# Token centring and the restoring product on quarters of the array, low band summed in PSUM

## The chip, the cores and the metric

The kernel runs on one core of one Trainium2 chip. The metric is device time in microseconds. Several runs of a kernel are given by their median; one further execution is taken by the profiler, and its trace is what the rows below are read from.

## The reference

Input x is (4, 64, 128, 128): batch, channel, height, width. Two blocks are computed, each a convolution part and a token part, each with a residual:

```python
x = x + L0_conv(_ln_c(x))          # Haar wavelet mixer        <- the stage that the change touches
t = to_tokens(x)
t = t + L0_ffn(_ln_t(t))           # expert-choice top-8 MoE   <- its gate logits come from the same stage
x = from_tokens(t)
x = x + L1_conv(_ln_c(x))          # four directional scans
t = to_tokens(x)
t = t + L1_ffn(_ln_t(t))           # top-2 mixture
```

`_ln_c` and `_ln_t` both normalise over the 64 channels of a pixel (eps 1e-6 and 1e-5). `L0_conv` takes the Haar transform of each 2x2 block into four bands, scales each by exp(s) per channel, projects the 256 band channels to 64 (w1, b1), projects back to 256 (w2, b2) and inverts the transform. The Haar transform, the scales and w1 are one linear map of the four pixels to the low projection (`Alow`); w2 and the inverse are another, back to the four pixels (`Brec`). With the weights that reach the kernel, the restored value depends on the row and column parity of the pixel.

## The kernel before

The image is cut into 64 chunks. A chunk is a tile of 128 partitions by 512 columns: partition halves t=0,1 are even and odd image rows, 64 channels each; columns are 4 row pairs by 128 pixels, so even and odd columns v=0,1 are neighbours. Per chunk `wavelet_mixer` does:

- `centre`: x split in two fp32r parts, times the centring matrix `Cm` (block diagonal: a 64x64 block for each half) into PSUM `xc`; `square` (ScalarE), split again (VectorE, GpSimd); `variance`: times `J` (1/64 in two diagonal blocks) into `va`; `log_of_variance`, `rstd` (ScalarE); `normalise` (VectorE) gives `nn`.
- `low`: for v=0,1, `Alow[:, v]` (128x64) times the columns of parity v, 256 of them. The two results lie in the two partition halves of bank `tv`, not yet summed; `copy_low` adds b1 (zero in the second half) and moves both to `lowS` (128x256).
- `restore`: for v=0,1, `Brec[:, v]` (128x128, both partition halves alike, so the product also sums the two parts of low) times `lowS` into `rec`. `add_restored` (VectorE, two instructions) adds it and b2 to x: the chunk then holds x1.
- `token_centre` (full `Cm` times x1 into `tc`) and `token_square` (ScalarE, into `tsq`); `turn` (four transposes of x1) and `copy_tokens` (VectorE), which is stored as token rows.
- Per pair of chunks `gate_logits` (into `lg`), `token_variance` (into `tv`, on column halves), `token_rstd` (two ScalarE instructions), `scale_logits` and `block_top` (VectorE).

f32 matmuls appear as two instructions each in the trace, fp32r ones as one.

All engines execute in order, in the order written out in the source; semaphores join them. Step c of the loop mixes chunks of different age. The order on each engine (in parentheses the lag, and "odd" for what stands only in odd steps):

- TensorE (455-469): centre(c), variance(c-1), low(c-2), odd: gate_logits and token_variance, then token_centre(c-3), turn(c-3), restore(c-2).
- ScalarE (508-520): square(c), log(c-1), copy_low(c-2), rstd(c-1), odd: token_rstd, then token_square(c-3).
- VectorE (588-602): add_restored(c-3), high_of_square(c), high_of_x(c+2), scale_logits or block_top, normalise(c-1), copy_tokens(c-3).
- GpSimd: low_of_square(c), low_of_x(c+2). SP: loads three steps ahead, stores of x1 and tokens.

`centre(c)` waits for `normed` of chunk c-2 (two `xc` banks); `copy_tokens` waits for `turn`; `low` and `token_variance` share bank `tv`. One loop over steps 0 to 68 runs them; odd steps are long, even ones short.

Of the kernel before, what the change touches and what calls it, by code (L numbers as in the profile page):

```python
# [30 lines left out]
P = 128  # L31
# [144 lines left out]
def setup_block0(nc, g, a):  # L176

    with ExitStack() as ctx:
# [21 lines left out]
        with nc.Block() as block:  # L200
            @block.sync
            def _(sp):
                def load(dst, src, sem):
                    sp.dma_start(dst, src, allow_slow_non_contiguous=True).then_inc(sem, 16)

                for h in range(2):
                    part = slice(h * C, h * C + C)
                    load(w2n[part, :, 0:C], a["w2"].rearrange("(j c) o -> c j o", j=4), loaded)
                    load(w1n[:, :, h], a["w1"].rearrange("o (j c) -> o j c", j=4), loaded)
                    load(gwn[:, h], a["gate_w"], loaded)  # L210
                for c in range(AHEAD):
                    for t in range(2):
                        sp.dma_start(g.xr[c][t * C:t * C + C].rearrange("p (j w) -> p j w", j=JR),
                                     x_chunk(a, c, t)).then_inc(g.xin[c], 16)
                load(g.b1[0:C], a["b1"].rearrange("(c o) -> c o", o=1), g.late_loaded)
                for q in range(4):
                    load(g.gate_b[q * E0:q * E0 + E0, :], a["gate_b"].rearrange("(e o) -> e o", o=1), g.late_loaded)
                load(g.w2bias, a["weight2"][:, HID:HID + 1, :].rearrange("e h o -> e (h o)"), g.late_loaded)
# [9 lines left out]
            def _(dve):  # L228
# [4 lines left out]
                dve.memset(g.eps[:, 0:1], EPS_C)  # L233
                dve.memset(g.eps[:, 1:2], EPS_T)
                dve.memset(gtb[:], 0.0)
                dve.memset(g.b1[C:P], 0.0)
                dve.memset(g.E[:, TOK:TOK + PAD], SENTINEL)
                dve.memset(sg[0:C], 1.0)
                dve.memset(sg[C:P], -1.0)
# [80 lines left out]
def wavelet_mixer(nc, g, a):  # L320
# [3 lines left out]
    with ExitStack() as ctx:  # L324
        m = Mem(nc, ctx, "wm")
        xc = [m.ps("xc0"), m.ps("xc1")]
        va, rec, tc, tt, lg, tv = (m.ps(n) for n in ("va", "rec", "tc", "tt", "lg", "tv"))
        xin, x1_out, tok_out = g.xin, m.sems("x1o", XBUFS), m.sems("tko", 4)
        s = {n: m.sem(n) for n in (
            "centred", "squared", "var", "lnv", "rstd", "normed", "low", "low_s", "rec", "x1",  # L330
# [11 lines left out]
        def now(c):  # L342

            return 0 <= c < CHUNKS

        def buf(c):

            return xr[c % XBUFS]

        with nc.Block() as block:  # L350
            @block.sync
            def _(sp):
                def load(c):
                    wait(sp, x1_out[c % XBUFS], c // XBUFS * 16)
                    wait(sp, s["tturned"], c - XBUFS + 1)
                    wait(sp, s["logits"], (c - XBUFS) // 2 * 2 + 2)
                    for t in range(2):
                        sp.dma_start(buf(c)[t * C:t * C + C].rearrange("p (j w) -> p j w", j=JR),
                                     x_chunk(a, c, t)).then_inc(xin[c % XBUFS], 16)

                def load_experts(q):

                    e = slice(q * E0 // 8, (q + 1) * E0 // 8)
                    sp.dma_start(g.W1[0:C + 1, e], a["weight1"][e].rearrange("e d h -> d e h")
                                 ).then_inc(g.experts_loaded, 16)
                    for t in range(2):
                        sp.dma_start(g.W2[:, e, t, :], a["weight2"][e, t * P:t * P + P, :].rearrange(
                            "e p o -> p e o")).then_inc(g.experts_loaded, 16)

                def store_x1(c):  # L370
                    wait(sp, s["x1"], c + 1)
                    sp.dma_start(g.x1s[c:c + 1].rearrange("t p n -> p (t n)"), buf(c)).then_inc(x1_out[c % XBUFS], 16)

                def store_tokens(c):
                    wait(sp, s["tcopied"], c + 1)
                    sp.dma_start(tok_dst[c % B][:, c // B * JR:c // B * JR + JR, :],
                                 ts[c % 4].rearrange("p (j x) -> p j x", j=JR)).then_inc(tok_out[c % 4], 16)

                for sem in g.setup_sems:
                    sp.sem_clear(sem)  # L380
                for c in steps:
                    if now(c + AHEAD):
                        load(c + AHEAD)
                    if 8 <= c < 16:
                        load_experts(c - 8)
                    if now(c - 3):
                        store_x1(c - 3)
                    if now(c - 4):
                        store_tokens(c - 4)
                for u in range(XBUFS):  # L390
                    sp.wait_ge(x1_out[u], 16 * len(range(u, CHUNKS, XBUFS)))
                for u in range(4):
                    sp.wait_ge(tok_out[u], 16 * (CHUNKS // 4))
                sp.wait_ge(g.late_loaded, 16 * 6)

            @block.tensor
            def _(pe):
# [14 lines left out]
                def low(c):  # L412
                    wait(pe, s["normed"], c + 1)
                    wait(pe, s["low_s"], c)
                    wait(pe, s["tln"], (c - 2) // 2)
                    nv = nn[c % 2].rearrange("p (q v) -> p v q", v=2)
                    for v in range(2):
                        last = pe.matmul(tv[v * C:v * C + C, 0:N // 2], g.Alow[:, v], nv[:, v], start=True, stop=True)
                    last.then_inc(s["low"], 1)

                def gate_logits(pair):
# [6 lines left out]
                def token_variance(pair, c):  # L428
                    wait(pe, s["tsquared"], 2 * pair + 2)
                    wait(pe, s["low_s"], min(c + 1, CHUNKS))  # L430
                    for half in range(2):
                        last = pe.matmul(tv[half * C:half * C + C, :], g.J[:, C - E0:C + E0], tsq[half],
                                         start=True, stop=True)
                    last.then_inc(s["tvar"], 2)

                def token_centre(c):
                    wait(pe, s["x1"], c + 1)
                    wait(pe, s["tsquared"], c)
                    pe.matmul(tc[:], g.Cm[:], buf(c), start=True, stop=True).then_inc(s["tcentred"], 1)

                def turn(c):
                    wait(pe, s["tcopied"], c)
# [4 lines left out]
                def restore(c):  # L447
                    wait(pe, s["low_s"], c + 1)
                    wait(pe, s["x1"], c)
                    for v in range(2):  # L450
                        last = pe.matmul(rec[:, v * (N // 2):(v + 1) * (N // 2)], g.Brec[:, v], lowS[c % 2],
                                         start=True, stop=True)
                    last.then_inc(s["rec"], 1)

                for c in steps:
                    if now(c):
                        centre(c)
                    if now(c - 1):
                        variance(c - 1)
                    if now(c - 2):  # L460
                        low(c - 2)
                    if now(c - 4) and c % 2 == 1:
                        gate_logits((c - 4) // 2)
                        token_variance((c - 4) // 2, c - 2)
                    if now(c - 3):
                        token_centre(c - 3)
                        turn(c - 3)
                    if now(c - 2):
                        restore(c - 2)
# [2 lines left out]
            def _(act):  # L472
# [15 lines left out]

                def copy_low(c):
                    if c == 0:  # L490
                        act.wait_ge(g.late_loaded, 16 * 6)
                    wait(act, s["low"], c + 1)
                    wait(act, s["rec"], c - 1)
                    act.activation(lowS[c % 2], tv[:, 0:N // 2], ACT.Identity, bias=g.b1[:]).then_inc(s["low_s"], 1)

                def token_rstd(pair):
                    wait(act, s["tvar"], 2 * pair + 2)
# [4 lines left out]

                def token_square(c):
                    wait(act, s["tcentred"], c + 1)
                    wait(act, s["tvar"], c - 1)
                    act.activation(tsq[c % 2], tc[:], ACT.Square).then_inc(s["tsquared"], 1)

                for c in steps:
                    if now(c):
                        square(c)  # L510
                    if now(c - 1):
                        log_of_variance(c - 1)
                    if now(c - 2):
                        copy_low(c - 2)
                    if now(c - 1):
                        rstd(c - 1)
                    if now(c - 4) and c % 2 == 1:
                        token_rstd((c - 4) // 2)
                    if now(c - 3):
                        token_square(c - 3)  # L520

            @block.gpsimd
            def _(pool):
# [18 lines left out]
            def _(dve):  # L542
# [6 lines left out]

                def add_restored(c):  # L550
                    wait(dve, s["rec"], c + 1)
                    xv = buf(c).rearrange("p (q v) -> p v q", v=2)
                    for v in range(2):
                        last = dve.scalar_tensor_tensor(xv[:, v], rec[:, v * (N // 2):(v + 1) * (N // 2)],
                                                        g.b2c[:, v:v + 1], xv[:, v], ALU.add, ALU.add)
                    last.then_inc(s["x1"], 1)

# [1192 lines left out]
def metaformer_kernel(nc, a, out):  # L1750
    g = Shared()
    with ExitStack() as ctx:
# [18 lines left out]

        v = Views(g.X, 0)
        g.xr = [v.take(N) for _ in range(XBUFS)]
        g.sq, g.rr, g.nn, g.tsq = ([v.take(N) for _ in range(2)] for _ in range(4))
        g.lowS = [v.take(N // 2) for _ in range(2)]
        g.ts = [v.take(N) for _ in range(4)]
        g.trs = v.take(N)
        v = Views(g.X, 2 * (TOK + PAD))
# [58 lines left out]
```

## Time and profile before

| | us |
|---|---|
| median of 3 runs (lowest, highest) | 2211.32 (2211.24, 2211.95) |
| time of the profiled execution | 2214.93 |
| its span, which the rows are relative to | 2213.0 |
| TensorE busy in the span | 2096.7 |

The wavelet stage lies between 15 and 336 us of the span. Three more stages follow (expert choice, four scans, mixture). A row of a timeline begins with the start in us and the duration in us of the instruction or of xN merged instructions; consecutive instructions of an engine overlap in their records, so the distance from start to start is often less than a duration.

### The profile page before, as it was taken

What the parts mean: (1) busy time and instruction counts of PE and PEld (TensorE: products, weight loads), DVE (VectorE), ACT (ScalarE), POOL (GpSimd) and SP (SyncE); (2) the same over time, 40 slices, a digit from 0 to 9 for tenths busy, and PEclk for the clock granted to TensorE, in tenths of its full rate; (3) what the DMA queues carried; (4) which work ended last, traced back from release to release, by engine and by line L of the source; (5) the groups of instructions that cost most, each with busy time, mean ns of one, the idle gap of its engine ahead of it and who ended that gap; (6) DMA issues with size and microseconds to landing.
All of it is one profiled execution on the core that took longest, in us unless ns stands there. A gap on an engine that the chain in (4) does not pass through costs nothing. (4 is left out here: it accounts for less than half of the span.)

```text
span 2213.0 us, 40957 instructions
## 1 busy us (share of the span) xinstructions
PE 2096.7 (95%) x14474; PEld 1611.6 (73%) x14474; DVE 1273.2 (58%) x2621; ACT 1037.5 (47%) x2879; POOL 590.6 (27%) x644
## 2 busy tenths in 40 slices
PE   6999991799999989999999999999996999999999
PEld 3555550477777789999999999999994555555554
DVE  4777778566666633222222222222226999999998
ACT  4666664344444313333444444444445455454451
POOL 4555534222222200000000000000006655656561
PEclk9999995699999999999999999999996999999999
DMA  4955540222223200000000000000004555555543
GB/s 114 240 166 163 167 142 22 91 86 93 90 96 96 68 12 0 0 0 0 4 0 0 0 0 0 0 0 0 0 0 118 129 131 131 132 131 130 128 117 77
DMA packets 176417, 159.06 MB, mean 72 GB/s; under 512 B 25976, under 2 KB 126360, under 8 KB 176280
## 3 DMA queue, kind: packets, MB, share of 16 engines
q1 hardware_dynamic: 174584, 156.91, 26.1%
q8 instruction: 61, 1.00, 0.2%
q0 software_dynamic: 512, 0.53, 0.1%
q14 instruction: 76, 0.62, 0.1%
q10 hardware_dynamic: 1184, 0.00, 0.0%
HBM read 56.72 MB, written 67.11 MB: 56 GB/s over the span
## 5 line engine op out<-in xcount | busy, mean ns | idle before, releaser
L1194 PE MATMUL s_ps<-g_ring,g_T 128*128 128x128 f32 x7620 | 855.4, 274 | 7.6 <-DVE g_ring L1237 7.6
L1194 PEld LDWEIGHTS s_ps<-g_ring,g_T 128*128 128x128 f32 x7620 | 854.5, 191 | 8.3 <-DVE g_ring L1237 8.1
L1226 DVE SCALAR_TENSOR_TENSOR g_ring<-s_ps,s_xs 128x128 f32<-128x128 f32 x508 | 148.3, 292 | 421.3 <-PE s_ps L1194 421.3
L1574 POOL TENSOR_TENSOR g_X<-tm_x,g_X 128x512 f32<-128x512 f32 x64 | 83.4, 1325 | 869.0 <-DVE tm_m L1654 869.0
L1282 ACT ACTIVATE g_X<-g_ring 128x256 f32<-128x256 f32 x254 | 172.2, 678 | 294.2 <-DVE g_ring L1226 294.2
L1663 DVE TENSOR_TENSOR tm_Z<-tm_pg,tm_nd 128x1024 f32<-128x1024 f32 x256 | 299.0, 1209 | 10.1 <-PE tm_pg L1457 10.0
L1469 PE MATMUL tm_po<-tm_Z,g_wexp 128*64 128x512 f32 x1024 | 247.7, 605 | 0.0
L1266 ACT ACTIVATE g_X<-g_ring 64x256 f32 x256 | 106.8, 417 | 205.6 <-DVE g_ring L1226 203.3
L1226 DVE SCALAR_TENSOR_TENSOR g_ring<-s_ps,g_X 128x128 f32<-128x128 f32 x254 | 74.0, 292 | 211.0 <-PE s_ps L1194 211.0
L1277 ACT ACTIVATE s_xs<-g_X 128x256 f32<-128x256 f32 x254 | 161.4, 637 | 0.6 <-PEq L1176 0.6
L1457 PE MATMUL tm_pg<-tm_gT,tm_sel 96*128 96x512 f32 x512 | 146.9, 408 | 1.1 <-DVE tm_Z L1663 1.0
L1469 PEld LDWEIGHTS tm_po<-tm_Z,g_wexp 128*64 128x64 f32 x1024 | 62.2, 136 | 108.5 <-issue 99.8
L997 PEld LDWEIGHTS af_ps<-g_yh,g_Tlo 128*128 128x128 f32 x635 | 85.0, 189 | 66.7 <-DVE g_yh L1108 54.2
L526 POOL TENSOR_TENSOR wm_sql<-g_X,wm_sqh 128x512 fp32r<-128x512 f32 x64 | 89.2, 1394 | 134.3 <-DVE wm_sqh L561 133.1
L997 PE MATMUL af_ps<-g_yh,g_Tlo 128*128 128x256 f32 x635 | 111.5, 306 | 5.9 <-DVE g_yh L1108 4.2
L1578 POOL TENSOR_TENSOR tm_xl<-g_X,tm_xh 128x512 fp32r<-128x512 f32 x64 | 82.9, 1296 | 98.8 <-ACT tm_xh L1503 98.7
L1457 PEld LDWEIGHTS tm_pg<-tm_gT,tm_sel 96*128 96x128 f32 x512 | 92.6, 190 | 20.4 <-issue 4.1
L1108 DVE SCALAR_TENSOR_TENSOR g_yh<-af_ps,g_X 128x256 fp32r<-128x256 f32 x127 | 54.0, 426 | 90.5 <-PE af_ps L1001 87.8
L1511 ACT ACTIVATE tm_nS<-tm_bankA 128x512 f32<-128x512 f32 x64 | 38.2, 596 | 140.9 <-PE tm_bankA L1424 140.9
L1001 PE MATMUL af_ps<-g_yl,g_Thi 128*128 128x256 f32 x635 | 99.2, 288 | 0.0
L997 PE MATMUL af_ps<-g_yh,g_Thi 128*128 128x256 f32 x635 | 97.9, 285 | 0.0
L1526 ACT ACTIVATE tm_bankA<-tm_bankA 128x64 f32<-128x64 f32 x256 | 53.4, 220 | 88.5 <-PE tm_bankA L1436 88.5
(279 smaller groups left out, 3140.4 us busy)
## 6 DMA issues: line engine op xcount, KB each, us to landing
tm_nd<-tm_nS SPq DMA_DIRECT2D x256, 128.0 KB, 2.4
g_X<-in_x SPq DMA_DIRECT2D x128, 128.0 KB, 3.0
x1s<-g_X SPq DMA_DIRECT2D x64, 256.0 KB, 2.1
x1tok<-g_X SPq DMA_DIRECT2D x64, 256.0 KB, 2.5
tm_x<-x2s SPq DMA_DIRECT2D x64, 256.0 KB, 2.9
y<-tm_yo SPq DMA_DIRECT2D x128, 128.0 KB, 2.5
g_X<-x1s SPq DMA_DIRECT2D x32, 256.0 KB, 2.8
x2s<-g_X SPq DMA_DIRECT2D x32, 256.0 KB, 2.0
```

What stands on the lines that cost most here:

```text
L526: pool.tensor_tensor(sq_lo[:], sq[c % 2], sq_hi[:].bitcast(F32), ALU.subtract).then_inc(s["parts"], 1)
L997: pe.matmul(out, t[:, d * P:d * P + P], g.yh[:, :, d:d + 64], start=(t is g.Tlo and d == 0), stop=False)
L1001: last = pe.matmul(out, g.Thi[:, d * P:d * P + P], g.yl[:, :, d:d + 64], start=False, stop=(d == ND - 1))
L1194: last = pe.matmul(out, g.T[i][:, d * P:d * P + P], g.ring[(u - 1) % RING][:, images(c), d:d + 64], start=(d == 0), stop=(d == ND - 1))
L1226: dve.scalar_tensor_tensor(g.ring[n % RING][:, images(c), inner], conv, 0.0, x[:, images(c)], ALU.max, ALU.add).then_inc(y_ready[c], 1)
L1266: last = act.activation(dst.rearrange("p b j w -> p b (j w)"), src, ACT.Copy)
L1277: act.activation(xs[n % RING][:], line(*place(n)), ACT.Copy).then_inc(staged, 1)
L1282: act.activation(line(*place(n)), g.ring[n % RING][:, :, inner], ACT.Copy).then_inc(stored, 1)
L1457: last = pe.matmul(pg[q % 2][:, h * N:h * N + N], sel[:, at:at + 2].rearrange("p e c -> p (e c)"), gT[i][:], start=True, stop=True)
L1469: last = pe.matmul(po[i][h * C:h * C + C, :], wexp[:, ep], Z[q % 4][:, h], start=False, stop=(ep == EP - 1), skip_group_check=True)
L1574: pool.tensor_tensor(xv, natural(x2[t % 2][i][:]), xv, ALU.add).then_inc(s["x3"], 1)
L1663: dve.tensor_tensor(Z[q % 4][:], pg[q % 2][:].rearrange("p (h n) -> p h n", h=2), nd[t % 2][i][:], ALU.mult).then_inc(s["z"], 1)
```

## The change

`token_centre` and `restore` issue 64x64 quarters; `low` sums over v in PSUM, with the column half h in the partitions, so `lowS` is 128x128; `rec` and `tc` share two banks (row groups write different banks). `token_variance` then has 16 instructions on 32-column strips. `tsq` has four buffers for two. On TensorE `token_centre` moves ahead of `low`, on ScalarE `token_square` moves ahead of `copy_low`.

```diff
-                load(g.b1[0:C], a["b1"].rearrange("(c o) -> c o", o=1), g.late_loaded)
+                for h in range(2):
+                    load(g.b1[h * C:h * C + C], a["b1"].rearrange("(c o) -> c o", o=1), g.late_loaded)
...
-                dve.memset(g.b1[C:P], 0.0)
...
-        va, rec, tc, tt, lg, tv = (m.ps(n) for n in ("va", "rec", "tc", "tt", "lg", "tv"))
+        va, tt, lg, tv = (m.ps(n) for n in ("va", "tt", "lg", "tv"))
+
+        both = m.ps("rt", (P, 2 * N))[:].rearrange("p (r k n) -> p r k n", r=2, k=2)
+        rec, tc = both[:, :, 0], both[:, :, 1]
...
                 def low(c):
...
-                    nv = nn[c % 2].rearrange("p (q v) -> p v q", v=2)
+                    nv = nn[c % 2].rearrange("p (h q v) -> p h v q", h=2, v=2)
                     for v in range(2):
-                        last = pe.matmul(tv[v * C:v * C + C, 0:N // 2], g.Alow[:, v], nv[:, v], start=True, stop=True)
+                        for h in range(2):
+                            last = pe.matmul(tv[h * C:h * C + C, 0:N // 4], g.Alow[:, v], nv[:, h, v],
+                                             start=(v == 0), stop=(v == 1))
...
                 def token_variance(pair, c):
-                    for half in range(2):
-                        last = pe.matmul(tv[half * C:half * C + C, :], g.J[:, C - E0:C + E0], tsq[half],
-                                         start=True, stop=True)
+                    for h in range(2):
+                        of_half = g.J[:, h * C:h * C + E0]
+                        for half in range(2):
+                            for t in range(2):
+                                at = half * C + t * E0
+                                last = pe.matmul(tv[at:at + E0, h * (N // 2):(h + 1) * (N // 2)], of_half,
+                                                 tsq[(2 * pair + half) % 4][:, t * (N // 2):(t + 1) * (N // 2)], start=True, stop=True)
...
                 def token_centre(c):
-                    pe.matmul(tc[:], g.Cm[:], buf(c), start=True, stop=True).then_inc(s["tcentred"], 1)
+                    src = buf(c).rearrange("p (h n) -> p h n", h=2)
+                    for t, h in ((0, 0), (1, 1), (0, 1), (1, 0)):
+                        rows = slice(t * C, t * C + C)
+                        last = pe.matmul(tc[h * C:h * C + C, t], g.Cm[rows, rows], src[rows, h], start=True, stop=True)
+                    last.then_inc(s["tcentred"], 1)
...
                 def restore(c):
                     wait(pe, s["low_s"], c + 1)
                     wait(pe, s["x1"], c)
+                    wait(pe, s["tsquared"], c)
                     for v in range(2):
-                        last = pe.matmul(rec[:, v * (N // 2):(v + 1) * (N // 2)], g.Brec[:, v], lowS[c % 2],
-                                         start=True, stop=True)
+                        for h, t in ((0, 0), (1, 1), (0, 1), (1, 0)):
+                            rows = slice(h * C, h * C + C)
+                            last = pe.matmul(rec[t * C:t * C + C, h, v * (N // 4):(v + 1) * (N // 4)],
+                                             g.Brec[rows, v, t * C:t * C + C], lowS[c % 2][rows], start=True, stop=True)
...
+                    if now(c - 3):
+                        token_centre(c - 3)
                     if now(c - 2):
                         low(c - 2)
                     if now(c - 4) and c % 2 == 1:
                         gate_logits((c - 4) // 2)
                         token_variance((c - 4) // 2, c - 2)
                     if now(c - 3):
-                        token_centre(c - 3)
                         turn(c - 3)
...
-                    act.activation(lowS[c % 2], tv[:, 0:N // 2], ACT.Identity, bias=g.b1[:]).then_inc(s["low_s"], 1)
+                    act.activation(lowS[c % 2], tv[:, 0:N // 4], ACT.Identity, bias=g.b1[:]).then_inc(s["low_s"], 1)
...
                 def token_square(c):
-                    wait(act, s["tvar"], c - 1)
-                    act.activation(tsq[c % 2], tc[:], ACT.Square).then_inc(s["tsquared"], 1)
+                    wait(act, s["tvar"], c - 3)
+                    act.activation(tsq[c % 4].rearrange("p (t n) -> p t n", t=2), tc, ACT.Square
+                                   ).then_inc(s["tsquared"], 1)
...
+                    if now(c - 3):
+                        token_square(c - 3)
                     if now(c - 2):
                         copy_low(c - 2)
                     if now(c - 1):
                         rstd(c - 1)
                     if now(c - 4) and c % 2 == 1:
                         token_rstd((c - 4) // 2)
-                    if now(c - 3):
-                        token_square(c - 3)
...
                 def add_restored(c):
-                    xv = buf(c).rearrange("p (q v) -> p v q", v=2)
+                    xv = buf(c).rearrange("p (h q v) -> p v h q", h=2, v=2)
                     for v in range(2):
-                        last = dve.scalar_tensor_tensor(xv[:, v], rec[:, v * (N // 2):(v + 1) * (N // 2)],
+                        last = dve.scalar_tensor_tensor(xv[:, v], rec[:, :, v * (N // 4):(v + 1) * (N // 4)],
                                                         g.b2c[:, v:v + 1], xv[:, v], ALU.add, ALU.add)
```

The views of the shared array X follow (`tsq` four tiles, `lowS` two of 128 columns), and two waits for the late loads count seven loads for six.

## Rows read from the trace of the kernel before

**Rows 1.** Page part 1, and windows of the stage: busy us of each engine, clock, DMA.

```profile
PE 2096.7 (95%) x14474; PEld 1611.6 (73%) x14474; DVE 1273.2 (58%) x2621; ACT 1037.5 (47%) x2879; POOL 590.6 (27%) x644
...
34.60:314.80 280.20, 280.20 (x1297) 156.30 (x1295) 209.42 (x411) 192.60 (x353) 154.28 (x118) 1.00 0.62 179
```

**Rows 2.** Timeline of TensorE over one pair of steps: start, duration, instruction.

```profile
148.91 0.58 PE L403 MATMUL wm_xc<-wm_xh,wm_Cmr 128*128 128x512 f32 x1
...
152.80 0.58 PE L403 MATMUL wm_xc<-wm_xh,wm_Cmr 128*128 128x512 f32 x1
...
153.45 0.39 PE L409 MATMUL wm_va<-wm_sqh,g_J 128*128 128x512 f32 x1
...
153.69 0.40 PE L410 MATMUL wm_va<-wm_sql,g_J 128*128 128x512 f32 x1
154.01 0.67 PE L418 MATMUL wm_tv<-g_X 128*64 128x256 f32 x4
...
154.52 1.02 PE L425 MATMUL wm_lg<-g_X 128*64 128x512 f32 x4
...
155.37 1.06 PE L432 MATMUL wm_tv<-g_X,g_J 128*64 128x512 f32 x4
...
156.36 1.13 PE L439 MATMUL wm_tc<-g_X,g_Cm 128*128 128x512 f32 x2
...
157.32 0.60 PE L444 MATMUL wm_tt<-g_X 128*128 128x128 f32 x4
...
158.44 0.58 PE L403 MATMUL wm_xc<-wm_xh,wm_Cmr 128*128 128x512 f32 x1
```

**Rows 3.** Timeline of VectorE and ScalarE in the same pair.

```profile
151.87 0.69 DVE L566 TENSOR_TENSOR g_X<-wm_xc,g_X 128x512 f32<-128x512 f32 x1
...
152.47 0.68 DVE L571 COPY g_X<-wm_tt 128x512 f32<-128x512 f32 x1
...
153.19 0.88 DVE L554 SCALAR_TENSOR_TENSOR g_X<-wm_rec,g_b2c,g_X 128x256 f32<-128x256 f32 x2
...
153.65 0.60 ACT L478 ACTIVATE g_X<-wm_xc 128x512 f32<-128x512 f32 x1 [1.17 <-PE wm_xc L404]
...
154.15 0.69 ACT L483 ACTIVATE g_X<-wm_va,g_eps 128x512 f32<-128x512 f32 x1
...
154.73 0.48 ACT L494 ACTIVATE g_X<-wm_tv,g_b 128x256 f32<-128x256 f32 x1
...
155.10 0.62 ACT L487 ACTIVATE g_X<-g_X 128x512 f32<-128x512 f32 x1
```

**Rows 4.** Timeline of the next stage around 64x64 quarters, weight loads (PEld) last.

```profile
500.42 0.40 PE L1031 MATMUL af_dl<-af_sql,g_J 128*128 128x512 f32 x1
500.75 0.68 PE L1021 MATMUL af_xc<-g_X,g_Cm 64*64 64x256 f32 x8
501.36 0.88 PE L997 MATMUL af_ps<-g_yh,g_Tlo 128*128 128x256 f32 x5
502.07 0.77 PE L997 MATMUL af_ps<-g_yh,g_Thi 128*128 128x256 f32 x5
502.68 0.78 PE L1001 MATMUL af_ps<-g_yl,g_Thi 128*128 128x256 f32 x5
...
500.75 0.21 PEld L1021 LDWEIGHTS af_xc<-g_X,g_Cm 64*64 64x64 f32 x8 [0.36 <-issue]
```

**Rows 5.** Expert stage: 32-column matmuls, and the window with its granted clock.

```profile
381.96 7.05 PE L881 MATMUL ec_psh<-g_X,ec_pT 65*32 65x256 f32 x64 [0.42 <-ACT ec_pT L808]
...
382.00:398.00 16.00, 14.30 (x208) 9.47 (x208) 15.96 (x5) 4.36 (x7) 7.79 (x4) 0.51 0.11 35
```

**Rows 6.** Timeline at the stage's end: a token centring that waits for VectorE.

```profile
328.92 0.88 DVE L554 SCALAR_TENSOR_TENSOR g_X<-wm_rec,g_b2c,g_X 128x256 f32<-128x256 f32 x2 [0.17 <-PE wm_rec L451]
...
329.85 1.12 PE L439 MATMUL wm_tc<-g_X,g_Cm 128*128 128x512 f32 x2 [0.97 <-DVE g_X L554]
```

**Rows 7.** Timeline of ScalarE at the stage's start: the first copy_low.

```profile
27.33 0.47 ACT L494 ACTIVATE g_X<-wm_tv,g_b 128x256 f32<-128x256 f32 x1 [0.43 <-PE wm_tv L418]
```

More of the change, by code:

```diff
@@ L393, in _ @@
                     sp.wait_ge(tok_out[u], 16 * (CHUNKS // 4))
-                sp.wait_ge(g.late_loaded, 16 * 6)
+                sp.wait_ge(g.late_loaded, 16 * 7)
             @block.tensor
@@ L490, in copy_low @@
                     if c == 0:
-                        act.wait_ge(g.late_loaded, 16 * 6)
+                        act.wait_ge(g.late_loaded, 16 * 7)
                     wait(act, s["low"], c + 1)
                     wait(act, s["rec"], c - 1)
-                    act.activation(lowS[c % 2], tv[:, 0:N // 2], ACT.Identity, bias=g.b1[:]).then_inc(s["low_s"], 1)
+                    act.activation(lowS[c % 2], tv[:, 0:N // 4], ACT.Identity, bias=g.b1[:]).then_inc(s["low_s"], 1)
                 def token_rstd(pair):
@@ L1773, in metaformer_kernel @@
         g.xr = [v.take(N) for _ in range(XBUFS)]
-        g.sq, g.rr, g.nn, g.tsq = ([v.take(N) for _ in range(2)] for _ in range(4))
-        g.lowS = [v.take(N // 2) for _ in range(2)]
+        g.sq, g.rr, g.nn = ([v.take(N) for _ in range(2)] for _ in range(3))
+        g.tsq = [v.take(N) for _ in range(4)]
+        g.lowS = [v.take(N // 4) for _ in range(2)]
         g.ts = [v.take(N) for _ in range(4)]
```

## The prediction

> **What bounds the kernel now.** The page comes first: TensorE is busy for 95% of the span [rows 1]. The windows then cut out the wavelet stage. From 34.6 to 314.8 us TensorE is busy for all 280.20 us, VectorE for 209.42, ScalarE for 192.60, GpSimd for 154.28 [rows 1]. So the array is the limit there and no other engine is. Next comes the timeline of TensorE. It repeats one pair of steps: a short one (148.91 to 152.80, 3.89 us) and a long one with the logits and the token variance (152.80 to 158.44, 5.64 us), 9.53 us together [rows 2]. Steps 4 to 63 are 30 such pairs, 286 us. Last I read ScalarE and VectorE in the same pair [rows 3], because once the array is shorter their order may be the next limit.
>
> **What the change takes off TensorE.** The logits are four matmul instructions of 512 columns that go two by two on the column halves, each in two passes: four pass times in 0.85 (154.52 to 155.37) [rows 2], 0.213 each. An f32 product on the full array takes four passes. The short step thus streams for 0.853 (centre and variance, one pass for each of four instructions) + 0.427 (low) + 0.853 (token centring) + 0.427 (turn) + 0.853 (restore) = 3.41; the long step 1.71 more, 5.12.
>
> Four 64x64 quarters at once halve the columns: 0.427 for the token centring. The next stage already does this very operation (L1021, 64*64, 64x256, x8), with 0.61 to the next start [rows 4], where the full one has 0.96 (156.36 to 157.32) [rows 2]. So quarters do run side by side. `restore` becomes sixteen 64*64 matmuls of 128 columns, 0.427 in place of 0.853. `low` issues eight for four, with the same columns. `token_variance` issues sixteen for four on 32-column strips, each strip 2x256 columns: 0.853 as before. L881, 64 matmuls of 32x256 in 7.05 us at a granted clock of 0.51 [rows 5], is 0.110 each, 0.055 at full clock; sixteen give 0.88. Streaming falls to 2.56 and 4.27.
>
> **What it adds on TensorE: changes of shape.** L1021 starts 0.33 after the last full matmul, where 0.235 is usual (153.45 to 153.69); the group stands for 0.18 over its streaming; and the five matmuls behind it take 0.71 where the next five take 0.61 [rows 2, 4]. In and out together cost 0.09+0.18+0.10 = 0.37 to 0.39, some 0.19 per change. Today a step has two changes. Afterwards it has five: to quarters (token centring), to column halves (low), to full (turn), to quarters (restore), to full; the long step has a sixth if 32-column strips count as another shape.
>
> In the new order of TensorE the short step is centre and variance 1.14 (4x0.235, +0.09 on leaving, +0.11 behind quarters), token centring 0.61, low 0.60 (the long step's 0.51 to a group of its own shape and 0.09 to another), turn 0.65 (0.427 and a change on either side), restore 0.61: 3.61. The long one has 0.51+0.85+0.99 for low, logits and token variance [rows 2] in place of 0.60: 5.36. A sixth change makes it 5.55; if changes between two tiled shapes are free it is 5.15. I take 5.36, since most of the changes are of the kind that [rows 4] shows.
>
> The Trainium skill, "TensorEngine Tiling (Array Packing)", section Key Properties, says that changing the tiling mode drains the array. [...]
>
> **What it moves: a ring closes.** Token centring now stands before `low`, and `token_square` before `copy_low` and `rstd` on ScalarE, where it was last. This makes a ring: x1 of a chunk, token centring, token square, copy_low, rstd, normalise, copy_tokens, add_restored, which is x1 of the next chunk. All of it lies within one step. With x1 at 0:
> - hop from VectorE's add to the centring 0.05 (328.92+0.88 to 329.85) [rows 6]; quarters to their end 0.68 [rows 4]; hop of the same size: square at 0.78.
> - ScalarE would be free at 0.78+0.50 (square to log, 153.65 to 154.15) [rows 3], 1.28. But `low` starts 0.61 behind the centring and ends 0.67 later [rows 2, 4], at 1.33; hop 0.05 (154.68 to 154.73) [rows 2, 3]: copy_low at 1.38.
> - copy_low: log (512 columns) 0.69 and copy_low (256) 0.48 have the same bias operand and give 0.82 ns a column [rows 3], so 0.37 for 128. Its successor starts 0.11 before its end [rows 3]: rstd at 1.64, and 0.62 later it ends, 2.26.
> - hop 0.05: normalise 2.31; copy_tokens 0.60 later, add 0.60 later (151.87 to 152.47 for an instruction of that length) [rows 3], 3.51; its two halves 0.88 [rows 3]: 4.39.
>
> The short step can't be under 4.39, though TensorE could do it in 3.61; it is 3.89 now. Queued behind the waiting centring on TensorE are low, turn and restore, and ScalarE's two copies wait with them; behind the waiting normalise stand copy_tokens and the add. The add reads PSUM in runs of 128 instead of 256, same elements: nothing, at most 0.05. Bounds for the ring: 4.25 if `low` doesn't gate and the hops shrink, 4.55 if split operands and eight weight loads slow it. `centre` of the next step also awaits this normalise (end 3.00), and centre plus variance then last until 4.14, just under 4.39.
>
> In the long step copy_tokens waits for `turn`, behind the token variance. From turn's start VectorE needs 0.60+0.05+0.60+0.88+0.05 = 2.18, TensorE 0.55+0.61+1.14 = 2.30, so TensorE sets it, at 5.36; were it quicker by over 0.12, VectorE would be next.
>
> The rest: restore's new wait for the token square adds nothing, as the square precedes the copy_low that restore awaits anyway. Four `tsq` buffers for two, one memset less: nothing. One more tiny load of b1 ahead of gate_b in SP's queue: the first copy_low comes at 27.33 [rows 7], long after; nothing.
>
> **Sum.** Pair: 4.39+5.36 = 9.75 against 9.53, +0.22; times 30, +6.6 us. At the start the first restores, issued alone, get shorter; at the end the last short steps, which have no centre, wait for the same ring. I set these against each other, with 1 us either way. The profiled execution has a span of 2213.0 and a time of 2214.93; it would give 2221.5. The median of the runs is 3.6 under it, so the forecast is 2211.3+6.6 = **2217.9**.
>
> **Rivals.**
> - A, no difference that shows (within 0.2%, 4.4 us, about what a measurement of this kernel can tell): changes between adjoining tiled shapes are free (long step 5.15) and the ring is 4.30 to 4.45. The pair is 9.45 to 9.60, the time 2209 to 2213. For it: only changes between full and tiled are in the trace. Against it: leaving quarters slows even the matmuls behind them.
> - B, faster: the ring doesn't bind, since some member has slack that I took for order. The pair is 3.61+5.36 = 8.97, -0.56 times 30: 2194; half of it, 2203. Against it: every member awaits the one before or follows it on its engine. It decides once the ring is under 4.0.
> - C, much slower: the sixteen loads and matmuls of restore don't overlap in the array and it keeps its 0.853. The long step is 0.43 more, 30 times: 2231. It decides if sixteen short ones behave otherwise than L1021's eight, whose loads lie within 0.21 us [rows 4].
> - D, the ring at 4.55 and the sixth change: pair 10.1, 2228.
>
> The Trainium skill, "TensorE: Matmul & The Clock Gate", section LDWEIGHTS, times a load by its columns over 1.2 GHz, 53 ns for 64. Sixteen in a row would be 0.85, which is C's size; that section doesn't say whether loads of different quarters share the time, and eight in 0.21 us say they do.
>
> **How the numbers follow.** Forecast 0.45, with a range of its own from 2213.5 to 2223; A 0.27; B 0.17; C 0.05; D 0.06. The range for 8 in 10 is 2205 to 2229: all of A and D, and only the mildest of B. Faster by over 0.2% (below 2206.9) is B with a trace of A, 0.18. Within 0.2% is A and the low edge of the forecast, 0.28. Slower 0.54.
>
> **What would show it.** Token centring as 64*64 x8 in about 0.6 us and restore as sixteen in the same; in every short step TensorE idle before token centring, released by VectorE's add, 0.2 to 0.6 us, and no such idle in long steps; copy_low at about 0.37 us, started by `low`. A short step clearly under 4.2 refutes the ring; a long step near 5.15 or 5.55 settles the changes of shape; restore above 0.8 shows that it doesn't overlap. The other stages must not move: if they do, or if the granted clock of this stage leaves 1.00, the forecast fails for another reason.

## The result

The changed kernel takes 2220.69 us (median of 5 runs, 2220.02 to 2223.28), the kernel before 2211.32 (5 runs, 2210.19 to 2213.92). The ratio is 1.0041, 95% interval 1.0029 to 1.0053: slower, by 9.4 us where 6.6 were forecast.

The page and the windows of the profile after (for windows: length, busy us of PE, PEld, DVE, ACT, POOL, granted clock, DMA share, GB/s):

```profile
PE 2073.7 (93%) x16266; PEld 1595.2 (72%) x16266; DVE 1268.6 (57%) x2620; ACT 1036.6 (47%) x2879; POOL 591.0 (27%) x644
...
34.60:314.80 280.20, 258.65 (x2868) 142.19 (x2872) 200.82 (x403) 188.08 (x346) 151.73 (x116) 1.00 0.62 178
```

TensorE is busy for 23 us less and the kernel is slower. In the stage it is no longer full: 258.65 of 280.20 us, against 280.20 [rows 1]. The clock of the stage did not move.

One short and one long step of TensorE, the timeline after (start, duration, instruction):

```profile
152.58 0.66 PE L451 MATMUL wm_rt<-g_X,g_Cm 64*64 64x256 f32 x8
...
153.17 0.67 PE L422 MATMUL wm_tv<-g_X 128*64 128x128 f32 x8
...
155.65 0.47 PE L406 MATMUL wm_xc<-wm_xh,wm_Cmr 128*128 128x512 f32 x1 [0.62 <-DVE g_X L584]
...
156.42 0.40 PE L413 MATMUL wm_va<-wm_sql,g_J 128*128 128x512 f32 x1
...
156.94 0.66 PE L451 MATMUL wm_rt<-g_X,g_Cm 64*64 64x256 f32 x8
...
158.04 1.03 PE L430 MATMUL wm_lg<-g_X 128*64 128x512 f32 x4
...
159.00 1.07 PE L441 MATMUL wm_tv<-g_X,g_J 128*32 128x256 f32 x16
...
160.00 0.66 PE L457 MATMUL wm_tt<-g_X 128*128 128x128 f32 x4
...
160.59 0.67 PE L467 MATMUL wm_rt<-g_X 64*64 64x128 f32 x16
...
161.18 0.50 PE L406 MATMUL wm_xc<-wm_xh,wm_Cmr 128*128 128x512 f32 x1
...
161.98 0.40 PE L413 MATMUL wm_va<-wm_sql,g_J 128*128 128x512 f32 x1
...
162.31 0.66 PE L451 MATMUL wm_rt<-g_X,g_Cm 64*64 64x256 f32 x8
```

From token centring to token centring the short step is 4.36 us (152.58 to 156.94), the long one 5.37 (to 162.31). The pair is 9.73 against 9.53 [rows 2]: 30 times +0.20 is 6.0 us. Start to start, token centring stands at 0.59 where the full one stood at 0.96 [rows 2]. Restore stands at 0.59 for 0.427 of streaming, so its sixteen matmuls do run side by side; what the quarters of restore gain once the changes of shape are paid is told below. Most of the rest of the stage's loss is at its end, also told below.

The members of the ring in that short step, VectorE and ScalarE, and the weight loads of the next token centring:

```profile
153.31 0.60 ACT L523 ACTIVATE g_X<-wm_rt 128x512 f32<-128x512 f32 x1
...
153.89 0.37 ACT L511 ACTIVATE g_X<-wm_tv,g_b 128x128 f32<-128x128 f32 x1
...
154.16 0.62 ACT L504 ACTIVATE g_X<-g_X 128x512 f32<-128x512 f32 x1
...
154.81 0.69 DVE L584 TENSOR_TENSOR g_X<-wm_xc,g_X 128x512 f32<-128x512 f32 x1 [0.60 <-ACT g_X L504]
155.42 0.68 DVE L589 COPY g_X<-wm_tt 128x512 f32<-128x512 f32 x1
...
156.02 0.87 DVE L572 SCALAR_TENSOR_TENSOR g_X<-wm_rt,g_b2c,g_X 128x256 f32<-128x256 f32 x2
...
156.94 0.21 PEld L451 LDWEIGHTS wm_rt<-g_X,g_Cm 64*64 64x64 f32 x8 [0.56 <-DVE g_X L572]
```

Square, copy_low (0.37), rstd, normalise, copy_tokens, add, and the token centring 0.05 behind the add's end. In every short step TensorE waits twice: `centre` waits 0.62 for normalise (155.65), and the token centring waits for the add. That second wait is 0.19: from the last variance to the token centring it is 0.52 (156.42 to 156.94), in the long step 0.33 (161.98 to 162.31). The forecast had put the whole idle time, 0.2 to 0.6 us, before the token centring; the larger part lies before `centre`, at the ring's own normalise. The bracket of a weight load is no sign by itself: in the long step it names the same add.

```profile
162.31 0.21 PEld L451 LDWEIGHTS wm_rt<-g_X,g_Cm 64*64 64x64 f32 x8 [0.36 <-DVE g_X L572]
```

### The profile page after: what moved, and what is told of

It is laid out like the page before. It is cut to its first block and busy times, and to the rows that moved or that the text cites. A ratio compares the mean times of both kernels' runs of the same rounds, so it can differ in the third digit from the quotient of the medians.

```text
span 2218.8 us, 44539 instructions
## 1 busy us (share of the span) xinstructions
PE 2073.7 (93%) x16266; PEld 1595.2 (72%) x16266; DVE 1268.6 (57%) x2620; ACT 1036.6 (47%) x2879; POOL 591.0 (27%) x644
```

## The experiments

Steps are read as above (token centring to token centring; centre to centre in the kernels with token centring behind low). The last column but one is where the last block_top of the stage starts in the profiled execution. Each ratio is to runs of the kernel before on the same chip. Where an expectation says "the first experiment", it means the changed kernel with add first.

| kernel | short | long | pair | stage's end | ratio (95%) |
|---|---|---|---|---|---|
| before | 3.89 | 5.64 | 9.53 | 335.4 | 1 |
| changed | 4.36 | 5.37 | 9.73 | 344.3 | 1.0041 (1.0029, 1.0053) |
| before, new order alone | 4.92 | 5.90 | 10.82 | 377.5 | 1.0190 (1.0173, 1.0207) |
| changed, order back | 3.97 | 6.31 | 10.28 | 359.8 | 1.0107 (1.0090, 1.0124) |
| same, square before token_rstd | 3.98 | 5.67 | 9.65 | 338.1 | 1.0011 (1.0002, 1.0021) |
| changed, add first | 4.17 | 5.37 | 9.54 | 336.3 | 1.0007 (0.9998, 1.0017) |
| before, add first | 3.89 | 5.64 | 9.53 | 335.6 | 0.9999 (0.9990, 1.0008) |
| changed, rstd first | 3.99 | 5.68 | 9.67 | 338.3 | 1.0019 (1.0009, 1.0028) |
| changed, rstd and add first | 4.09 | 5.38 | 9.47 | 332.6 | 0.9999 (0.9989, 1.0008) |
| changed, turn early | 4.36 | 5.51 | 9.87 | 348.8 | 1.0062 (1.0046, 1.0077) |
| changed, full restore | 4.46 | 5.55 | 10.01 | 351.7 | 1.0081 (1.0066, 1.0096) |
| add first, variance first | 3.93 | 5.36 | 9.29 | 328.5 | 0.9976 (0.9967, 0.9984) |
| same, rstd first | 3.93 | 5.54 | 9.47 | 333.6 | 1.0002 (0.9993, 1.0010) |

### The new order without the quarters

```diff
 # kernel before, TensorE; likewise token_square ahead of copy_low on ScalarE, and four tsq buffers
+                    if now(c - 3):
+                        token_centre(c - 3)
                     if now(c - 2):
                         low(c - 2)
...
                     if now(c - 3):
-                        token_centre(c - 3)
                         turn(c - 3)
```

> The kernel before with the order move alone: full-array token centring ahead of low, token_square ahead of copy_low, four tsq buffers; no quarters. Ring theory: the ring has the full centring (0.96 to low's start) and the 256-column copy_low (0.37 to its successor): 0.05+0.96+0.67+0.05+0.37+0.62+0.05+0.60+0.60+0.88 = 4.85 for the short step, the long one 5.64; pair 10.5 against 9.53, 30 times +0.96: about 2240. Rival, the quarters and their changes of shape cost the time and the order nothing: 2211.

Measured: 2256.75 us, 42.7 over the runs of before. About 2240 was expected. The short step is 4.92 (4.85 expected). So the order by itself makes the loss, and far more of it with full centring: the quarters earn back most of what the order costs. The long step is 5.90, not 5.64, a miss. There too the token centring waits for the add, and the add for restore's end:

```profile
153.44 1.03 PE L451 MATMUL wm_rec<-g_X 128*128 128x256 f32 x4
...
154.51 0.88 DVE L555 SCALAR_TENSOR_TENSOR g_X<-wm_rec,g_b2c,g_X 128x256 f32<-128x256 f32 x2 [0.17 <-PE wm_rec L451]
...
155.44 1.13 PE L439 MATMUL wm_tc<-g_X,g_Cm 128*128 128x512 f32 x2
```

Restore ends at 154.47, the add runs from 154.51 to 155.39, and the centring starts at 155.44.

### The quarters in the old order

```diff
 # changed kernel: on TensorE token_centre back in front of turn; on ScalarE:
-                    if now(c - 3):
-                        token_square(c - 3)
                     ...copy_low, rstd, token_rstd
+                    if now(c - 3):
+                        token_square(c - 3)
```

> The changed kernel with the order of before on TensorE and ScalarE, quarters kept. Ring theory: the ring opens, but restore now waits for token_square, which in long steps stands behind both token_rstd instructions: token variance's end +0.05+0.72+0.53+0.60 against restore's natural place, a stall of 0.8; short step 3.9 (token_square last, 0.3 stall). Pair 9.9 to 10.0: about 2227, so the move was needed by the shared banks. Rival, the order move is all of the loss: short 3.6, long 5.4 to 5.55, pair 9.1, 2201.

> As the order of before with quarters, but token_square ahead of token_rstd on ScalarE. Ring theory: no ring, small stall of restore for token_square: short step 3.9, long 5.45, pair 9.35, 30 times -0.38 from the changed kernel: about 2209. Rival, order is indifferent and shape changes are the cost: 2221.

Measured: 2238.57 and 2216.24, beside 2214.06 of before. The first is slower than the changed kernel, as expected, by more than expected (about 2227). In the long step restore waits for the token square, which stands behind both halves of token_rstd:

```profile
155.27 0.66 PE L451 MATMUL wm_rt<-g_X,g_Cm 64*64 64x256 f32 x8
155.41 0.69 ACT L515 ACTIVATE g_X<-wm_tv,g_eps 128x512 f32<-128x512 f32 x1 [0.99 <-PE wm_tv L441]
...
156.13 0.63 ACT L517 ACTIVATE g_X<-g_X 128x512 f32<-128x512 f32 x1
...
156.66 0.58 ACT L522 ACTIVATE g_X<-wm_rt 128x512 f32<-128x512 f32 x1
157.38 0.67 PE L467 MATMUL wm_rt<-g_X 64*64 64x128 f32 x16 [0.87 <-ACT g_X L522]
```

Since rec and tc share banks, the old order isn't open to the new layout as it stands. With the square ahead of token_rstd the long step falls from 6.31 to 5.67, and the kernel to 0.1% over before; I expected 5.45 and a gain, and missed what was left of the wait for the square (0.22 in front of restore) and the sixth change of shape. The Trainium skill, "PSUM — Partial Sum Buffer", section PSUM bank collisions raise a hardware error, says that two engines may not use one bank and quadrant at once even at different bytes; no run here shows it. Restore without its wait for the square was therefore not tried, and whether it would pay stays open.

### Which members close the ring

```diff
 # changed kernel, VectorE
-                    if now(c - 3):
-                        add_restored(c - 3)
                     if now(c):
                         high_of_square(c)
...
                         normalise(c - 1)
+                    if now(c - 2):
+                        add_restored(c - 2)
                     if now(c - 3):
                         copy_tokens(c - 3)
```

> The changed kernel with one edit on VectorE: add_restored(c-2) stands behind normalise(c-1) and ahead of copy_tokens(c-3), instead of behind it. Ring theory: copy_tokens' 0.60 leaves the ring; the ring is 3.79 and the short step 3.8 instead of 4.37, the long step stays 5.36 (TensorE). Pair 9.15 against 9.73, 30 times -0.57: about 2203 us, faster than both kernels. Rival, the changes of shape alone make the kernel slower (TensorE bound in both steps): nothing moves, 2221. Rival, another wait of the same length takes over: short step stays above 4.2, 2216 or more.

> Control: the kernel before with VectorE's add_restored(c-2) ahead of copy_tokens(c-3), the edit of the first experiment. TensorE is the limit in both steps of that kernel, so it gains nothing: the same within 0.2%. Rival, this order is better by itself and the first experiment's gain says nothing of a ring: 5 us or more faster than before.

Measured: 2215.5 (10 runs) beside 2214.06, and 2211.61 beside 2211.96. The edit is worth 0.3% on the changed kernel and nothing on the one before, so its gain is the ring's. But the short step is 4.17, not 3.79: the prediction had named the runner-up itself (normalise, centre and variance, token centring: 4.14), and this expectation left it out. The one wait that the waits of TensorE's matmuls in the stage name (who waited for whom, us in total, times, longest):

```profile
PE wm_xc L406 <- DVE g_X L584: 18.6, 30, 0.6
```

30 waits of 0.6 us of the next `centre` for normalise: one for each short step. The changed kernel has the same line; there the token centring then waits 0.19 more for the add, and here it follows the variance at once. So a second ring of 4.17 stood 0.2 us behind the first, and took over.

```diff
 # changed kernel, ScalarE; in the second kernel with the VectorE edit, and copy_low ahead of token_square
                         log_of_variance(c - 1)
+                    if now(c - 1):
+                        rstd(c - 1)
                     ...token_square, copy_low
-                    if now(c - 1):
-                        rstd(c - 1)
```

> The changed kernel with rstd(c-1) moved on ScalarE ahead of token_square(c-3) and copy_low(c-2), in this order; nothing else. Ring theory: both rings lose token square and copy_low, but copy_low now ends 2.24 behind the token centring and restore waits for it: short step 4.03 against 4.37; in the long step token_variance waits for copy_low (shared bank), 5.5 against 5.36. Pair 9.55 to 9.6, about 2216. Rival, the ring goes only through token square and low, and rstd's place is indifferent: 2221.

> The changed kernel with add_restored ahead of copy_tokens on VectorE (as in the first experiment) and, on ScalarE, rstd(c-1) right behind log_of_variance(c-1), then copy_low(c-2), then token_square(c-3). The first experiment's short step was 4.17 instead of 3.79 because a second ring took over: token square, copy_low, rstd, normalise, the next centre, variance, token centring. With rstd early neither ring contains it; what is left is restore waiting for the token square (2.24 behind the centring's start) and then restore 0.60, centre and variance 1.12: short step 4.0, long 5.36, pair 9.4. Second-ring theory: 30 times -0.17 from the 9.54 of the first experiment, 5 us under it, about 0.1 to 0.2% under the kernel before. Rival, TensorE or VectorE is the limit already at 9.54: no change from the first experiment.

Measured: 2214.72 and 2211.84 beside 2211.96. Alone, rstd first gives 3.99 and 5.68 (4.03 and 5.5 expected): both rings shorten, and copy_low, now later, holds up restore and in long steps the token variance. With both edits the pair is 9.47 (9.4 expected); in short steps restore then waits 0.51 for the token square, which stands last. Between the changed kernel and this one nothing but order differs, and the pair goes from 9.73 to 9.47: the order sets the time, and TensorE's sum is only a floor.

### What a change of shape costs

```diff
 # changed kernel, TensorE
+                    if now(c - 3):
+                        turn(c - 3)
                     if now(c - 4) and c % 2 == 1:
                         gate_logits((c - 4) // 2)
                         token_variance((c - 4) // 2, c - 2)
-                    if now(c - 3):
-                        turn(c - 3)
```

> The changed kernel with turn(c-3) ahead of the logits and the token variance in long steps, so that TensorE has one more change of shape there (column halves, full, column halves) and no work more. Theory of the changes of shape: the long step, which TensorE sets, grows by 0.15 to 0.2; short steps stay; 30 times +0.17: about 2226. Rival, changes cost nothing where weight loads can be drawn ahead: 2221. Rival, the long step is set by copy_tokens behind turn on VectorE, which now starts 2 us sooner: below 2219.

> The changed kernel with low, copy_low, restore and add_restored of before (full array, 256-column lowS); token centring stays on quarters, and the order stays. Two changes of shape less, restore's streaming 0.427 more. By the changes of shape as the profile after shows them (0.10 to 0.15 each) the long step grows by 0.13 to 0.23; the short step is the ring, which gets 0.10 longer by copy_low: 4.47. Pair 9.73 + 0.28: 8 us above the changed kernel, 2229. Rival, changes at 0.20 each as forecast: the long step is the same, the pair +0.13, 2225. Rival, quarters of restore are the cost: faster than the changed kernel.

Measured: 2225.49 beside 2211.96, and 2230.35 beside 2211.09. One more change adds 0.14 to the long step and nothing to the short one (4.36), so the long step is TensorE's. With a full restore two changes fall away, 0.427 of streaming returns, and the long step is 0.18 longer, as expected. But that long step is no longer TensorE's alone. The full restore ends later, the add waits for it, and the token centring for the add:

```profile
154.04 1.03 PE L463 MATMUL wm_rt<-g_X 128*128 128x256 f32 x4
...
154.72 0.58 PE L406 MATMUL wm_xc<-wm_xh,wm_Cmr 128*128 128x512 f32 x1
...
155.11 0.88 DVE L567 SCALAR_TENSOR_TENSOR g_X<-wm_rt,g_b2c,g_X 128x256 f32<-128x256 f32 x2 [0.18 <-PE wm_rt L463]
...
155.61 0.40 PE L413 MATMUL wm_va<-wm_sql,g_J 128*128 128x512 f32 x1
...
156.05 0.66 PE L449 MATMUL wm_rt<-g_X,g_Cm 64*64 64x256 f32 x8
```

The add ends at 155.99. From the last variance to the token centring it is 0.44, against the 0.33 of the changed kernel's long step, so 0.11 of the 0.18 is this wait and 0.07 is TensorE's. By this estimate the two changes gave back 0.427 less 0.07, 0.36 us, or 0.18 each, near the 0.19 of the forecast; that the expectation's 0.10 to 0.15 each gave the right step is luck. The added change cost 0.14, of another pair of shapes; whether the kind of change sets its price stays open. So the two changes around restore take back most of what its quarters save in streaming. What is left is 0.07 on TensorE and 0.11 by an earlier end of restore in long steps. The short step is 0.10 longer in this kernel, all of it in copy_low's 256 columns (0.47 for 0.37), which belong to the old form of `low`.

### A version that beats both

```diff
 # add first, and on TensorE
-                    if now(c):
-                        centre(c)
                     if now(c - 1):
                         variance(c - 1)
+                    if now(c):
+                        centre(c)
 # and on ScalarE
-                    if now(c):
-                        square(c)
                     if now(c - 1):
                         log_of_variance(c - 1)
+                    if now(c):
+                        square(c)
```

> The first experiment (add_restored ahead of copy_tokens) with variance(c-1) ahead of centre(c) on TensorE and log_of_variance(c-1) ahead of square(c) on ScalarE. Two-ring theory: the second ring (normalise, centre, variance, token centring) loses the variance, since only centre waits for normalise: normalise ends at 3.00 behind the token centring, centre 0.47+0.1 later gives 3.65; the first ring is 3.79 to 3.84. The split of the square (VectorE, then GpSimd, 1.40) must reach the variance earlier and may hold it until 2.80, which gives 3.9. Short step 3.85 to 3.9 against 4.17, long 5.38: pair 9.25, about 8 us under the first experiment and 0.2 to 0.3% under the kernel before. Rival, GpSimd's part becomes the limit: short step 4.2 or more, no gain over the first experiment.

> As the experiment beside it, but ScalarE in the order log, square, rstd, token_square, copy_low. Neither ring holds token square and copy_low; restore waits for copy_low, 2.18 behind the token centring, and then 0.60+1.12 and the changes of shape: short step 3.95. In long steps the token variance waits for copy_low by 0.1 to 0.2: 5.5. Pair 9.45, as the kernel of rstd first and add first, 3 to 6 us above the experiment beside it. Rival, with variance first ScalarE's order is indifferent: equal to it.

Measured: 2206.75 (11 runs) beside 2211.09, ratio 0.9976 (0.9967 to 0.9984), and 2212.09. The first is 0.24% faster than before and some 0.6% faster than the changed kernel, on the same work. Its short step is 3.93, and what ends it is GpSimd's part of the square's split, which holds variance until 2.81 behind the token centring (156.13 to 158.94; 2.80 expected):

```profile
157.49 1.40 POOL L544 TENSOR_TENSOR wm_sql<-g_X,wm_sqh 128x512 fp32r<-128x512 f32 x1 [2.73 <-DVE wm_sqh L579]
...
158.94 0.50 PE L412 MATMUL wm_va<-wm_sqh,g_J 128*128 128x512 f32 x1 [0.36 <-POOL wm_sql L544]
```

The second kernel has the same short step (3.93; 3.95 expected), where restore now waits 0.29 for copy_low, and loses in the long one (5.54; 5.5 expected), where the token variance waits for the late copy_low.

## Why the prediction was right, step by step

- **The ring.** 4.39 forecast, 4.36 measured, each member at its place. The order move alone (4.92 against 4.85), the order back (no ring) and the add first bear it out. This step carries the sign of the result. TensorE's idle time was foreseen in the wrong place, as told above.
- **The streaming saved.** Quarters at 0.59 to the next start, 0.61 forecast; rival C (no overlap) is out, as restore's sixteen stand at 0.59.
- **Changes of shape.** The long step came out at 5.36 to 5.37 as forecast, in part because errors cancel. Its terms by start to start: logits to token variance stands at 0.96, where 0.85 was taken from the kernel before, so the change to 32-column strips does cost 0.11 and there are six changes and not five. Against it, turn stands at 0.59 for 0.65, and token centring and restore at 0.59 for 0.61 each. Neither rival value of the long step came, 5.15 (A, changes between tiled shapes free) or 5.55 (D, a sixth at full price).
- **VectorE's runner-up in long steps** (0.12 behind) held, though closer than forecast: the add ends at 162.20, 0.11 before the token centring, and with the hop of 0.05 it is some 0.06 behind. With turn early, which frees copy_tokens, the long step did not fall; with a full restore this path took over.
- **The sum's ends.** This is the term that was mis-sized: 0 forecast with 1 us either way, +2.9 in the profile (8.9 less the 6.0 of the pairs). From the last centre to the last block_top it takes 23.3 us (321.0 to 344.3), before 20.7 (314.8 to 335.4); the other 0.3 lies before it. The windows after:

```profile
330.00:333.00 3.00, 1.10 (x14) 0.36 (x12) 2.52 (x5) 0.04 (x1) 0.00 (x0) 0.87 0.09 32
333.00:336.00 3.00, 3.00 (x20) 1.27 (x24) 0.00 (x0) 0.93 (x2) 0.00 (x0) 0.56 0.47 149
336.00:339.00 3.00, 2.00 (x40) 1.11 (x32) 1.70 (x4) 1.32 (x2) 0.00 (x0) 1.00 0.00 0
```

and what TensorE did there:

```profile
331.98 0.94 PE L451 MATMUL wm_rt<-g_X,g_Cm 64*64 64x256 f32 x8 [1.90 <-DVE g_X L572]
...
332.84 1.12 PE L422 MATMUL wm_tv<-g_X 128*64 128x128 f32 x8
...
333.76 1.92 PE L430 MATMUL wm_lg<-g_X 128*64 128x512 f32 x4
...
335.60 1.07 PE L441 MATMUL wm_tv<-g_X,g_J 128*32 128x256 f32 x16
```

The last short step has neither centre nor variance, so TensorE idled for 1.90 us, until the ring's add. From 333 to 336 us the granted clock was 0.56, near the lower of its two levels (1.2 GHz), and token centring, low and logits stood at 0.86+0.92+1.84 where 0.59+0.51+0.96 is usual: 1.6 us. The rest, 1.0 us, goes to the ring itself, in the last short steps (4.36 from 327.62 to 331.98, where the two of the kernel before took 3.4). In the kernel before the same place kept 1.00 (0.97 of idle in front of its last centring [rows 6]). That the idle time caused the drop is inferred; no run varied it alone. The other traces only partly bear it out. With turn early the same place idled for 1.91 us, and the clock of the next 3 us was 0.53. With a full restore it idled for 1.49 and with add first for 1.31, and the clock kept 1.00. But in the quarters with the order back the clock fell to 0.50 behind an idle time of 0.99, after other waits of 0.39 and 0.87 in front of restore. So the length of this one wait doesn't settle it.
- **The stage and the whole.** The stage ends 8.9 us later in the profile, the medians differ by 9.4, but the two spans only by 5.8 (2213.0 and 2218.8). The profiled execution before was itself 3.6 over its median; behind the stage, with the same code in both, the profile after gets 3 us back, 1.4 of it in the first scan (359.1 us from its first to its last convolution, against 360.5). Why these stages vary by that much isn't settled.

Rival B had its worth: a pair under 9.4 is possible (9.29), but only after the ring is opened in two places.

## What to carry to other kernels

When one engine is full, work out what it would take without it: follow each value from its producer back to its own next turn through every engine's order, and write down the second longest ring beside the first, as it stands there once the first is opened. Moving an operation ahead in one engine's order can close such a ring inside one step; here that was worth +1.9% with the operation at full size. Small tiles save streaming time, but count the changes of shape on either side of each group: around restore, two of them took back an estimated 0.36 of the 0.427 us saved.

## What the runs showed of the hardware

- Four 64x64 quarters run side by side, also with sixteen matmuls of 128 columns each and their sixteen weight loads: 0.59 us to the next group's start for 0.427 of streaming.
- One more change between array shapes with no work added cost 0.14 us; two fewer gave back 0.36 by estimate (0.427 of streaming returned, TensorE's part of the step grew by 0.07).
- Sixteen matmuls on 32-column strips, 256 columns each, stood at 1.00 us (159.00 to 160.00), as four on column halves did at 0.99 [rows 2]; finer cutting of the same columns cost nothing there, but the group in front, the logits, stood at 0.96 for 0.85.
- VectorE's add from PSUM in two runs of 128 columns across two banks took 0.87 to 0.88 for both halves, as with one run of 256 [rows 3].
